# Attention block: the output projection two steps earlier, the last tile's correction on VectorE, the sigmoid table loaded last

## The reference, cut to what matters

```
x = x + _L0_attn_ref(_layernorm(x), Wq, bq, Wk, bk, Wv, bv, Wo, bo, gq, gk)

attn = softmax(einsum('bhqd,bhkd->bhqk', q, k) * scale)
out  = einsum('bhqk,bhkd->bhqd', attn, v)      # 32 heads of 128
return out @ Wo + bo

def _layernorm(x): return (x - mean(x)) / sqrt(var(x) + 1e-5)
```

## Time and profile before

| | |
|---|---|
| time, median of 3 runs | 2248.1 us (2246.44 to 2248.6) |
| the profiled execution: its own time | 2247.08 us |
| its span in the trace | 2245.3 us |
| mean granted TensorE clock | 0.997 of full speed |
| TensorE busy | 98% of the span |
| VectorE, ScalarE, GpSimd busy | 79%, 56%, 35% |

### The profile page before, as it was taken

How to read it: one execution, slowest core, us unless ns; L and a number is a source line. 1 busy time by engine, 2 the same in 40 slices (tenths; PEclk the granted TensorE clock), 3 DMA queues, 4 the chain that set the end, 5 groups by cost and what they waited for, 6 DMA issues and landing times. The chain is left out here.

```text
span 2245.3 us, 34788 instructions
## 1 busy us (share of the span) xinstructions
PE 2198.2 (98%) x10852; PEld 1827.6 (81%) x10852; DVE 1766.9 (79%) x2873; ACT 1261.4 (56%) x2136; POOL 784.2 (35%) x698
## 2 busy tenths in 40 slices
PE   7999999999999999999999999999998999899998
PEld 6778888888788888888888888888886788688887
DVE  5787667676688888888888888888875699785897
ACT  3465555555566666666666666666655344572442
POOL 3586666665312222222122122222214410473110
PEclk9999999999999999999999999999999999999999
DMA  4165566655421212212212112122111121141211
GB/s 137 34 221 185 203 207 203 202 201 181 138 74 54 84 56 70 84 42 84 75 51 84 57 69 84 42 84 75 52 34 39 52 80 31 35 133 38 90 47 38
DMA packets 108488, 210.48 MB, mean 94 GB/s; under 512 B 9984, under 2 KB 42752, under 8 KB 107136
## 3 DMA queue, kind: packets, MB, share of 16 engines
q1 hardware_dynamic: 108416, 209.58, 28.1%
HBM read 140.33 MB, written 69.21 MB: 93 GB/s over the span
## 5 line engine op out<-in xcount | busy, mean ns | idle before, releaser
L1715 ACT ACTIVATE at_pT_hi<-ps 128x512 fp32r<-128x512 f32 x512 | 278.4, 596 | 354.6 <-PE ps L1839 354.6
L1772 DVE TENSOR_REDUCE softmax<-ps 128x1 f32<-128x1024 f32 x254 | 310.2, 1221 | 83.8 <-PE ps L463 83.0
L1783 DVE TENSOR_TENSOR at_pT_lo<-ps,at_pT_hi 128x512 fp32r<-128x512 f32 x512 | 327.2, 680 | 2.0 <-ACT at_pT_hi L1715 2.0
L463 PE MATMUL ps<-ln_xT_hi,first_parts 128*128 128x512 f32 x656 | 219.6, 396 | 6.7 <-PEq L1944 2.2
L463 PE MATMUL ps<-ln_xT_hi,queries 128*128 128x512 f32 x816 | 221.0, 390 | 0.0
L1796 DVE SCALAR_TENSOR_TENSOR x<-ps,softmax,x 128x512 f32<-128x512 f32 x256 | 192.1, 750 | 9.1 <-PE ps L463 4.2
L463 PE MATMUL ps<-ln_xT_hi,ln_xT_lo 128*128 128x512 f32 x768 | 196.0, 390 | 0.0
L1654 POOL TENSOR_TENSOR at_o_lo<-at_o_raw,at_o_hi 128x512 fp32r<-128x512 f32 x32 | 41.4, 1294 | 431.5 <-ACT at_o_hi L1737 431.5
L1864 PE MATMUL ps<-at_pT_hi,ln_xT_lo 128*128 128x512 f32 x512 | 180.6, 393 | 0.6 <-DVE at_y_lo L1768 0.6
L463 PEld LDWEIGHTS ps<-ln_xT_hi,queries 128*128 128x128 f32 x816 | 153.2, 188 | 32.6
L463 PEld LDWEIGHTS ps<-ln_xT_hi,ln_xT_lo 128*128 128x128 f32 x768 | 144.2, 188 | 30.7
(11 more groups left out here) (353 smaller groups left out, 5672.0 us busy)
## 6 DMA issues: line engine op xcount, KB each, us to landing
scratch_v<-v_res SPq DMA_DIRECT2D x64, 256.0 KB, 2.3
scratch_q_hi<-qkv_q_hi SPq DMA_DIRECT2D x64, 256.0 KB, 2.2
scratch_q_lo<-qkv_q_lo SPq DMA_DIRECT2D x64, 256.0 KB, 2.6
scratch_k<-qkv_res SPq DMA_DIRECT2D x64, 256.0 KB, 3.2
keys<-scratch_k SPq DMA_DIRECT2D x32, 512.0 KB, 3.7
at_v_raw<-scratch_v SPq DMA_DIRECT2D x32, 512.0 KB, 3.3
wv_raw<-in_Wv SPq DMA_DIRECT2D x8, 1024.0 KB, 6.1
queries<-scratch_q_hi SPq DMA_DIRECT2D x16, 512.0 KB, 3.7
```

The lines of the kernel that those rows point to most:

```text
L463: last = nc.tensor.matmul(out, s, m, start=(start and n == 0), stop=(stop and n == len(terms) - 1), skip_group_check=more)
L1715: nc.scalar.activation(pT2[jp][0][:, 4 * b:4 * b + 4, w * P:(w + 1) * P], T_BANKS[:, b * HALF:(b + 1) * HALF].rearrange("p (k n) -> p k n" ...
L1772: nc.vector.reduce_max(maxes[:, l % 4:l % 4 + 1], scores(l)[:], AX.X).then_inc(s_max, count(i, l))
L1783: nc.vector.tensor_tensor(pT2[jp][1][out], T_BANKS[:, b * HALF:(b + 1) * HALF].rearrange("p (k n) -> p k n", k=4), pT2[jp][0][out], ALU.su ...
```

## The change

The output projection and VectorE's addition of it run ten steps behind the scores instead of twelve (`WO_LAG`), so the first projection of a group comes in the very step in which its `y` is split. The drain has ten steps instead of twelve, and its ScalarE order is rewritten: the last split of `y` stands ahead of the step's other work one step earlier. The last tile's variance and Newton correction move from GpSimd to VectorE (`last_factor`, three fused operations for the four), the next block's first products are issued later, and the load of the sigmoid table moves behind the last high part.

```
-    T_LAG, PV_LAG, OUT_LAG, WO_LAG = 2, 6, 10, 12
+    T_LAG, PV_LAG, OUT_LAG, WO_LAG = 2, 6, 10, 10
...
 (GpSimd)
                     ln.newton(pool, final(i, l))
-                    ln.variance(pool, final(i, l))
+                    if final(i, l) < NT - 1:
+                        ln.variance(pool, final(i, l))
             steps(pool, step)
-            ln.newton(pool, NT)
...
 (ScalarE)
+            def y_high(i, l):
+                J, jp, _, _ = lagging(i, l, OUT_LAG)
+                act.wait_ge(s_pv, J + 1)
+                wait(act, s_wo, 4 * (J - 1))
+                nc.scalar.activation(y2[jp][0][:], core.bank(PV_BANK), ACT.Copy).then_inc(s_y_hi, 1)
+
             def step(i, l):
-                if l % 4 == OUT_LAG % 4 and exists(i, l, OUT_LAG):
-                    (the same three lines)
+                if l % 4 == OUT_LAG % 4 and exists(i, l, OUT_LAG) and final(i, l) != Y_AT:
+                    y_high(i, l)
+                if final(i, l) == Y_AT - 1:
+                    y_high(i, l + 1)
...
             def last_head(k):
-                if k == Y_AT:
-                    ln.scaled(act, k - 2)
-                    ln.root(act, k - 1)
-                    ln.centred(act, k - 1)
-                if k >= 2:
+                if k == Y_AT - 1:
+                    ln.root(act, k)
+                if k >= 1:
                     ln.high(act, k + 1)
                     ln.scaled(act, k - 1)
-                ln.root(act, k)
-                ln.centred(act, k)
+                if k < NT - 1:
+                    if k != Y_AT - 1:
+                        ln.root(act, k)
+                    ln.centred(act, k)
             steps(act, step)
+            act.wait_ge(last_var, 1)
+            nc.scalar.activation(ln.sd[:, NT - 1:NT], ln.var[:, NT - 1:NT], ACT.Sqrt).then_inc(ln.s_sd, 1)
+            ln.centred(act, NT - 1)
+            ln.high(act, NT + 1)
+            ln.scaled(act, NT - 1, last_rstd, 1)
+            ln.high(act, NT + 2)
             nc.scalar.preload_act_table(ACT.Sigmoid)
-            ln.high(act, NT + 1)
-            ln.scaled(act, NT - 1)
-            ln.high(act, NT + 2)
...
 (VectorE)
-                        if final(i, l) >= 2:
-                            ln.low(v, final(i, l) - 2)
+                        if final(i, l) >= 3:
+                            ln.low(v, final(i, l) - 3)
+            def last_factor():
+                c = slice(NT - 1, NT)
+                v.wait_ge(ln.s_aggr, NT)
+                nc.vector.tensor_scalar(ln.var[:, c], ln.meanvar[:, c, 1], LN_EPS, None, ALU.add)\
+                    .then_inc(last_var, 1)
+                ln.low(v, NT - 3)
+                ln.vector_first(v, NT)
+                ... (three operations: corr = var*r0, corr = 0.5*corr*r0, rstd = (corr - 1.5)*r0)
             steps(v, step)
-            ln.vector_first(v, NT)
+            last_factor()
...
 (TensorE)
                     ln.transposed(pe, k - 2)
-                    if k >= NT - 2:
-                        ln.first_part(pe, 0, 2 * (k - NT + 2), 2 * (k - NT + 3))
             steps(pe, step)
+            ln.first_part(pe, 0, 0, KB)
             ln.transposed(pe, NT - 2)
-            ln.first_part(pe, 1, 0, KB)
+            ln.first_part(pe, 1, 0, KB // 2)
             ln.transposed(pe, NT - 1)
+            ln.first_part(pe, 1, KB // 2, KB)
```

More of the change, by code:

```diff
@@ L1565, in attention_block @@
         s_wo, s_added = sem("wo_done"), sem("added")
+        last_var, last_corr, last_rstd = (sem(n) for n in ("last_var_done", "last_corr_done", "last_rstd_done"))
         prefetch = Prefetch(core, ctx, "at", following)
@@ L1740, in step @@
                 k = final(i, l)
-                if k is not None and k != Y_AT - 1:
+                if k is not None:
                     last_head(k)
             def last_head(k):
-                if k == Y_AT:
-                    ln.scaled(act, k - 2)
-                    ln.root(act, k - 1)
-                    ln.centred(act, k - 1)
-                if k >= 2:
+                if k == Y_AT - 1:
+                    ln.root(act, k)
+                if k >= 1:
                     ln.high(act, k + 1)
                     ln.scaled(act, k - 1)
-                ln.root(act, k)
-                ln.centred(act, k)
+                if k < NT - 1:
+                    if k != Y_AT - 1:
+                        ln.root(act, k)
+                    ln.centred(act, k)
             steps(act, step)
+            act.wait_ge(last_var, 1)
[4 more added lines that the diff above has]
+            ln.high(act, NT + 2)
             nc.scalar.preload_act_table(ACT.Sigmoid)
-            ln.high(act, NT + 1)
-            ln.scaled(act, NT - 1)
-            ln.high(act, NT + 2)
         @block.vector
@@ L1802, in step @@
                         ln.moments(v, final(i, l))
-                        if final(i, l) >= 2:
-                            ln.low(v, final(i, l) - 2)
+                        if final(i, l) >= 3:
[7 more added lines that the diff above has]
+                ln.vector_first(v, NT)
+                v.wait_ge(ln.s_r0, NT)
+                nc.vector.tensor_tensor(ln.corr[:, c], ln.var[:, c], ln.r0[:, c], ALU.mult).then_inc(last_corr, 1)
+                v.wait_ge(last_corr, 1)
+                nc.vector.scalar_tensor_tensor(out=ln.corr[:, c], in0=ln.corr[:, c], scalar=0.5, in1=ln.r0[:, c],
+                                               op0=ALU.mult, op1=ALU.mult).then_inc(last_corr, 1)
+                v.wait_ge(last_corr, 2)
+                nc.vector.scalar_tensor_tensor(out=ln.rstd[:, c], in0=ln.corr[:, c], scalar=-1.5, in1=ln.r0[:, c],
+                                               op0=ALU.add, op1=ALU.mult).then_inc(last_rstd, 1)
             steps(v, step)
-            ln.vector_first(v, NT)
+            last_factor()
             for t in (NT - 2, NT - 1):
```

## The result

The changed kernel takes 2253.49 us (median of 10 runs, 2250.86 to 2254.86) against 2247.76 us (10 runs, 2245.49 to 2248.77) for the kernel before on the same chip. The ratio is 1.0026, with a 95% interval of 1.0017 to 1.0034. That is +5.7 us, just beyond the 0.2% line; +4.9 was predicted. The profiled execution takes 2253.36 us with a span of 2251.4.

What follows compares the result with a forecast made beforehand. TensorE, busy throughout the steady part, was taken as the bound, so only the drain could gain. Steady +6.7 and drain -1.8 gave +4.9 us: 2252.0 from the profiled execution, 2253.0 predicted as median; range 2248.8 to 2255.6.

Steps and rivals of the forecast that it cites:

- 29 places late for the projection: Steady part: `at_y_lo` ends 0.16 to 0.17 us (14 groups) or 0.07 to 0.08 us (15) after the projection's load starts.
- Price, lateness plus L: Steady part: each late place costs its lateness plus L, from `at_y_lo`'s end to TensorE's load, 0.11 us; sum +6.7 us.
- the reading of a register may be done ahead of the wait: Loop step 2: reason given for keeping 0.11 us there despite a register instruction between wait and matmul.
- the bound from the earlier trace: Loop step 2: VectorE rows show 0.09 us more with a register instruction; at the 14 places the steady sum becomes 8.0.
- first rival: Steady part: TensorE's weight load overlaps the matmul ahead, hiding the wait; not slower, 2246.3 to 2249.8 us, chance 0.17.
- The other rivals: Drain gains nothing, 2255.5 us (chance 0.10); all 60 splits pay, 2260 us (0.03); faster by over 0.2% (0.03).
- First group: nothing: First split of `y`: TensorE waits for the same `at_y_lo` in the same step in both kernels, so no cost.
- Drain -1.8: End of attention: last addition 2 us earlier, then the table load last; net -1.8 us, bounds -2.4 to -1.2.
- Correction on VectorE: nothing: Drain: VectorE's three-operation correction of the last tile lies under early products, so moving it costs and gains nothing.
- The table load holds the barrier: End of drain: the 1.28 us table load comes last and the next block starts 0.27 us after it.
- Sum +4.9: Whole kernel: steady part +6.7 us and drain -1.8 us, bounds +1.1 to +6.8 us.
- What would show it: Changed trace: some 29 TensorE waits for `at_y_lo` at the projection, 0.28 and 0.19 us each, 6 to 7 us in all.

Runs made afterwards that it cites:

- experiment 1: Changed kernel with ScalarE's split of the next head's keys moved from loop steps 1 and 9 to 3 and 11: 2246.24 us, 0.9989 of before.
- experiment 4: Changed kernel with one, then two, added ScalarE copies ahead of the high part of y at the 30 remainder-6 places: 2253.34 us, then 2258.13 us.
- experiment 3: Changed kernel with one added ScalarE copy ahead of the high part of y at the 29 remainder-2 places: 2257.79 us, 1.0037 of before.
- keys_later_after: Changed kernel with the keys' split at loop steps 3 and 11 instead of 1 and 9: 2246.24 us, 0.9989 of before.
- experiment 6: Changed kernel, keys' split moved, one tail edit undone each: early products back 2246.50 us, last tile's correction on GpSimd 2244.81, no table load at the end 2244.43.
- lag_alone: Kernel before with the projection ten steps behind the scores and only the ScalarE drain order this needs: 2255.67 us, 1.0032 of before.
- the three with a delay: Changed kernel with added ScalarE copies ahead of the high part of y: one at remainder 2, 2257.79 us; one or two at remainder 6, 2253.34 or 2258.13.

## Why the prediction was right, step by step

- **29 places late for the projection: right.** 14 + 15 of them wait, the 30 of remainder 6 don't. Moving the keys takes all 29 away (experiment 1), so the cause named, the split ahead of the high part, is shown and not only argued.
- **Price, lateness plus L, 6.7 us: 0.4 too much, because L is not one number.** I took 0.11 for both kinds. It is 0.12 at loop step 2 and 0.05 at step 10: 14 x (0.17 + 0.12) + 15 x (0.075 + 0.05) = 5.9, measured 6.30 (4.18 at the 14 places, where 3.9 was predicted, 2.05 at the 15, where 2.8 was). The 0.4 between 5.9 and 6.30, about 0.01 us a place, no row explains. The term that was mis-sized is thus the second, the price of the 15 places. The two rows from which L came were read as "three waits on one matmul". The trace has an instruction of the sequencer there that carries the wait for `at_y_lo` by itself (experiment 4). So 0.11 held for places with such an instruction and was carried over to 15 places without one. The step "the reading of a register may be done ahead of the wait" failed too: the register instruction carries the wait and costs 0.07 over a wait on the matmul (the bound from the earlier trace rows said 0.09 over 0.11, which was too much). That 0.11 came so close to 0.12 at step 2 is luck.
- **A late load could lie under the matmul ahead (first rival): did not come.** In experiment 3 every added 0.20 us of lateness cost 0.20 us. The Trainium skill, "TensorE: Matmul & The Clock Gate", section "Step-by-step: what each phase is for", has weight loads pulled ahead of running matmuls and does not speak of a load that waits for a semaphore. Here such a load starts 0.05 or 0.12 us after the low part's end, and nothing covers the wait. Two figures of this rival were off: the sign would have turned at 0.17 us of cover, not 0.22 (6.7 - 29 x 0.17 = 1.8), and the transpositions ahead follow each other at 0.11 us, not 0.06.
- **The other rivals did not come either.** The drain gained (a net 1.44 at least); the 30 places of remainder 6 do not wait, so not all splits pay; and the kernel was not faster.
- **First group: nothing: right.** It waits in the same step in both kernels; the head's +1.32 is the two projections.
- **Drain -1.8: mechanism right, size right but for the clock.** From the last but one split's end the additions were foreseen at 1682.2, 84.2, 86.2, 88.7, 92.7, 95.0, 97.2 and 99.5. Taking off the 8.45 us by which that split ends later (1689.51 against 1681.06), the trace of the changed kernel has 82.1, 84.2, 86.2, 88.7, 92.7, 95.0 and 97.2, and then 1700.25 instead of 99.5. The granted clock of 0.53 and 0.62 is the difference: in keys_later_after, with the same drain and the clock whole, the last addition comes at 99.4 and the net is -1.9, in the changed kernel -1.44.
- **Correction on VectorE: nothing: right** (experiment 6). **The table load holds the barrier: right**, 0.59 us. The Trainium skill, "ScalarE: Activation LUTs", section "What ACT_TABLE_LOAD costs", adds a drain of about 1380 ns to the load. No such drain shows: the load starts 0.02 us behind the last high part, and the next block's first instruction comes 0.27 us behind the load, as the earlier trace rows.
- **Sum +4.9: the trace has +4.86** over attention. That it agrees so closely is luck: the price was 0.4 too high and the drain's gain 0.4 too high, the latter only because the clock fell in the profiled execution. With the clock whole the same parts give 6.3 - 1.9 = +4.4. The median's +5.7 holds 0.9 more, within the interval of +3.8 to +7.6; the stretches outside attention differ by as much between executions of one kernel.
- **What would show it: said too simply.** The waits were to be named for `at_y_lo` in TensorE's rows. At step 2 the load's idle time of 0.29 us is put down to "issue", at step 10 none is shown; the distances and the count of matmuls show the waits.

Left open: what the shorter lag alone does to the drain with the clock whole, and why the clock fell in some executions.

## What to carry to other kernels

When a consumer is moved closer to its producer, compare, at every step of the loop and for each kind of step, the producer's end with the consumer's slot; a lateness of 0.08 to 0.17 us and a hand-over of 0.05 to 0.12 at 29 places of the engine that bounds the kernel cost 6.3 us, of which the idle column shows 0.75. Then look at what stands directly ahead of the producer in its own engine's queue: here one line that moved the keys' split by two steps took the whole loss back. At the end of a block ask of every instruction on the last engine whether it must be done before the barrier; the table load, left to the next block, was hidden there.

## What the runs showed of the hardware

- Where the wait sat on the matmul itself, its weight load started 0.05 us after VectorE's instruction ended (15 places of the steady part); where it sat on an instruction of the sequencer ahead of it, 0.12 us (14 places). It is the same in all five traces with these waits (after, lag_alone and the three with a delay); the two such places of the kernel before show 0.11 to 0.12.
- In the drain the granted clock fell to the lower level in 4 of the 13 profiled executions that are in the table beside the kernel before, at different places (between 1695 and 1710). One kernel showed it in one execution and not in another, with 1.8 us between them (44.89 against 43.08); the changed kernel's drain was 0.56 longer than the same drain without it (42.07 against 41.51). The busy time just ahead of it did not decide it: 2.24 of 4 us in one drain in which it fell and in one in which it did not. What does, these runs do not tell.
- TensorE's busy share hides waits of 0.12 and most of those of 0.29 us, since the end of the transposition ahead is modelled beyond its slot: 6.3 us lost read as 0.75 us idle. The count of matmuls in a fixed stretch shows them (5475 against 5507).
